# The second mixture of a gated four-layer block: eight dense experts replaced by 30 row tiles sorted by expert

## The chip, the cores and the metric

The kernel runs on one core of a Trainium2 chip. Its engines have programs of their own and meet at semaphores: TensorE (PE; its weight loads appear as PEld), VectorE (DVE), ScalarE (ACT), GpSimd (POOL), and SyncE (SP), which issues most of the DMAs in the order of its program. The metric is the device time of one execution in microseconds (us), the median of several.

## The reference

The input x has 4 batches of 256 tokens with 256 features (1024 tokens, eight row blocks of 128). Four layers follow each other; each adds a gated attention and a gated feed-forward part:

```
for l in 0..3:
    x = x + tanh(g_xattn[l]) * xattn_l(layernorm(x), ctx)
    x = x + tanh(g_ffn[l])   * ffn_l(layernorm(x))
```

The feed-forward part of layer 2 is the *second mixture* (all in f32, 8 experts, inner width H = 256, each token goes to its best 2):

```
r       = x * rsqrt(mean(x^2) + 1e-6) * rsqrt(256) * router_scale
logits  = r @ router_logits                      # 1024 x 8
choices = top 2 of logits; weights = probs / sum of the two chosen probs
for each token and each of its two experts e:
    y_e = (gelu(x @ gate_e) * (x @ up_e)) @ linear_e * per_expert_scale[e]
out = sum of weights_e * y_e
```

Only 2 of the 8 experts of a token enter the result. The attention of layer 3 (L3X) has self and cross parts; the feed-forward part of layer 3 is the last mixture, with 16 experts of inner width 128.

## The kernel before

Each engine has one long program, written out by hand, and the order of the work on an engine is the order of the code. An attention is a loop over steps t (from -8 on), run by `attention(f, fill)` on each engine; work of other stages is put beside it by a callback `fill(t)` that says at which step it stands. L2X, the attention of layer 2, has 64 units (steps 0 to 63 and some steps behind for what is late), L3X 128. SP's queue is in order too: an issue that waits for a semaphore holds back everything behind it.

The second mixture, L2F, is dense. `turn_part` (PE L1179) transposes the normed rows of a batch, `logits` (L1364) gives router logits of all 1024 tokens, DVE's `top2_mask` and `topk_weights` turn them into a weight for each token and expert. Then `experts` (PE L1374) computes all eight experts for all tokens. Each operand is split in two parts in a rounded format (hi and lo), and a product takes three matmuls (hi*hi, lo*hi, hi*lo). `first` (L1377, matmul L1392) makes gates and ups of an expert in 48 matmuls of 512 columns, `second` (L1399, matmul L1408) its down product in 48 matmuls of 256 columns. ACT applies the gelu (L2127), DVE multiplies (L2838) and adds each expert's share to x (L2853). Weights arrive by SP's `expert_weights` (L702) into two slots: a load waits until the matmuls of the expert before the last are done (`refill_first`, L720). POOL splits them (`split_weights`, L988; L1004 and L1007 for hi and lo). The norms that open L3X (`begin_late` on each engine, `part_moments`, `late_norms` on DVE) follow the last expert's sums, two of them between them.

The last mixture already works on rows sorted by expert, and its functions are the model of the new code. POOL scatters each row of the normed input by an indirect DMA to a place in a list per expert (`scatter`, L1142); the places come from ranks (PE matmuls, DVE `places`, L3328 to L3335). SP loads tiles of 128 rows from the lists (`rows`, L828), which are 260 wide: 256 features, the token's number, its first expert, its two weights. For each of 31 tiles PE transposes the rows (`tile_turn`, L1772), multiplies with f32 weights (`tile_gates`, L1790; `tile_down`, L1800), ACT copies, applies the gelu and weights the result (`tile_copy` L2449, `tile_gelu` L2459, `tile_out` L2469), DVE multiplies (`tile_prod`, L3438 to L3441) and POOL scatters the outputs (L1156). The 16 first tiles have an expert each; 15 later ones take expert and list block from registers that DVE's `tile_map` (L3406) fills. SP's loop there is

```
for j in range(TILE_RING, TILES):
    sp.wait_ge(fs["l3f"]["y_added"], YR + j - TILE_RING + 1)
    rows(j)
    if j - TILE_RING < LATER:
        later_weights(j - TILE_RING)
```

In L2X other work is put in: roundings of the next attention's weights (`HIGH_SELF`: eight on ACT, L2324, eight on DVE, L3198), the parked query weights of L3X (`park`), keys and values of the context (`keys_values`, PE L1218, called kv units: eight of them stand in the opening of L3X), and `low_self` on POOL, which splits L3X's output weights beside the experts. `keep_clock` (L1168) issues transposes that nothing reads.

Of the kernel before, what the change touches and what calls it, by code (L numbers as in the profile page):

```python
# [20 lines left out]
P = 128  # L21
# [161 lines left out]
L2F = Ffn("l2f", 2, 8, 128, 2, ACT.Gelu_apprx_tanh, False)  # L183
L3F = Ffn("l3f", 3, 2, 128, 1, ACT.Gelu, True, (8, 32, 32))
# [17 lines left out]
KV_LATE_AT = ((-6, -4, -3), (-5, -4, -4, -3, -3, -2))  # L202
# [22 lines left out]
PARTS = ((0, 4), (4, 6), (6, 8))  # L225
HIGH_SELF = [("k", 0, slice(0, 1024)), ("k", 1, slice(0, 1024)), ("q", 0, slice(0, 1024)), ("q", 1, slice(0, 1024)),
# [4 lines left out]
def build(nc, T, out, we_dram, kv_first, kv_cross, rows_in, rows_out, cross_q):  # L231
    ctx = ExitStack()
    with ctx:
# [73 lines left out]
        with ExitStack() as a:  # L307
            sb("tile_w_low_hold", [P, 64 * 256], where=a)
            tile_w += [sb(f"tile_w{i}", [P, n_w], where=a) for i in range(10, 15)]
            sb("more_w_low_hold", [P, 16 * 256 - 5 * n_w], where=a)  # L310
            more_w += [sb(f"more_w{i}", [P, n_w], where=a) for i in range(5, 10)]
        w_high, w_low = ({n: sb(f"w{n}_{part}", shape, F32R) for n, shape in wshapes} for part in ("high", "low"))
# [44 lines left out]
        with ExitStack() as a:  # L357

            with ExitStack() as a2:
                act_hi = [sb(f"act_hi{i}", [P, 2, NTOK], F32R, where=a2) for i in range(2)]  # L360
                act_lo = [sb(f"act_lo{i}", [P, 2, NTOK], F32R, where=a2) for i in range(2)]
# [123 lines left out]

        ps = [ctx.enter_context(nc.psum_tensor(f"ps{i}", [P, HALF], F32)) for i in range(8)]
# [34 lines left out]
        for f in (L1F, L2F):  # L521
            fs[f.name] = {k: sem(f"{f.name}_{k}") for k in
                          ("w13_in0", "w13_in1", "w2_in0", "w2_in1", "w13_split", "w2_split", "gu_ready",
                           "gated_ready", "prod_done", "hi_ready", "act_ready",
                           "y_ready", "y_added") if not (f is L1F and k == "y_added")}
        fs["l3f"] = {**fs["l2f"], "w13_hi": sem("l3f_w13_hi"), "w2_hi": sem("l3f_w2_hi")}
# [17 lines left out]
        n_keys = len(L2X.loads) + len(L3X.loads)  # L544

# [65 lines left out]
        def _(sp):  # L611
# [56 lines left out]
            def attention_weights(c):  # L668
# [17 lines left out]
                elif 14 <= c < 18:  # L686
                    quarter_of("o", c - 14, 1, lw["wo_in"])
# [13 lines left out]

            def expert_weights(f, free, value):  # L702

                s = fs[f.name]
                w13d, w2d = T[f.name + "_w13"], T[f.name + "_w2"]

                def w13_load(slot, e):
                    sp.dma_start(w13[slot][:, 0:KB * 2 * f.F * f.FB], w13d[bass.ds(e, 1)].rearrange(
                        "e p n -> p (e n)")).then_inc(s[f"w13_in{slot}"], 16)

                def w2_load(slot, e):
                    sp.dma_start(w2[slot][0:f.F, 0:f.FB, :], w2d[bass.ds(e, 1)].rearrange(
                        "e p k d -> p (e k) d")).then_inc(s[f"w2_in{slot}"], 16)

                sp.wait_ge(free, value)
                for slot in range(2):
                    w13_load(slot, slot)
                    w2_load(slot, slot)

                def refill_first(e):  # L720

                    slot = e[1]
                    sp.wait_ge(s["gu_ready"], (e[0] * 2 + slot + 1) * f.units)
                    w13_load(slot, e[0] * 2 + slot + 2)

                def refill_second(e):
                    slot = e[1]
                    sp.wait_ge(s["y_ready"], (e[0] * 2 + slot) * 4 + 4)
                    w2_load(slot, e[0] * 2 + slot + 2)


                refill_first((0, 0))
                with sp.Fori(0, f.E // 2 - 2) as i:
                    refill_first((i, 1))
                    refill_second((i, 0))
                    refill_first((i + 1, 0))
                    refill_second((i, 1))
                refill_first((f.E // 2 - 2, 1))
                refill_second((f.E // 2 - 2, 0))
                refill_second((f.E // 2 - 2, 1))  # L740

# [73 lines left out]
            def routed_weights():  # L815

                sp.wait_ge(lw["wo_lo"], 5)
# [5 lines left out]
            def routed_rows():  # L823
# [15 lines left out]
                sp.wait_ge(placed, 16 * CHOICES * NT)  # L839
# [15 lines left out]
            def load_got():  # L855

                for i in range(4):
                    sp.wait_ge(y_put[i], 16 * ((TILES + 3 - i) // 4))
                for t in range(0, NT, 2):
                    sp.dma_start(got[t // 2][:, t % 2, :, :], rows_out[t * P * CHOICES:(t + 1) * P * CHOICES, :].rearrange(  # L860
                        "(p k) d -> p k d", k=CHOICES)).then_inc(got_loaded(t)[0], 16)

# [10 lines left out]
            key_load(L2X, 4)  # L873
            key_load(L2X, 5)
            park(1)
            values_load(2)
            key_load(L2X, 6)
            park(2)
            key_load(L2X, 7)
            park(3)  # L880
            park(4)
            values_load(3)
            for p in range(5, PARKS):
                park(p)
            expert_weights(L2F, layer_done, 5)
# [29 lines left out]
        def _(pool):  # L915
# [139 lines left out]
            def low_self(i):  # L1055

                for h in range(8 * (i - 1), 8 * i, 2):
                    low = low_output(wsets[1]["o"], slice(h, h + 2), 1)
# [2512 lines left out]
```

## Time and profile before

| what | us |
|---|---|
| median of three runs (1389.11 to 1389.65) | 1389.5 |
| span of the profiled execution (no other time of it is recorded) | 1393.2 |
| L2X, end of it: last output matmuls | 612.3 |
| second mixture: first to last expert matmul | 620.4 to 755.9 |
| first scores of L3X | 788.0 |
| last mixture's tiles | 1320.6 to 1376 |

The span is cut in stages at these times. A row of the stage view gives, for each stretch, the busy time of every engine with its number of instructions, the clock granted to TensorE (1.00 is 2.4 GHz, 0.50 is 1.2 GHz), the mean busy share of the 16 DMA engines and the rate in GB/s. The profile's page counts 1301.3 us of TensorE busy (93% of the span), 986.2 of DVE, 817.6 of ACT and 683.2 of POOL. Its share of the chain that ended last is 73% for TensorE. An f32 matmul appears as two instructions, a transpose as one. In a timeline row the text in brackets tells how long the engine idled before and what ended that.

### The profile page before, as it was taken

To read this page: it belongs to the slowest core of one execution; us is meant where nothing else is said; L and a number is where in the kernel's file an instruction comes from. 1 tells how busy PE (TensorE), PEld (TensorE's weight loads), DVE (VectorE), ACT (ScalarE), POOL (GpSimd) and SP (SyncE) were. 2 spreads that over 40 slices of the span, in tenths; PEclk is the share of its full clock that TensorE was granted. 3 is DMA by queue.
4 is the path that set the end of the run, shared out by engine and by line. 5 is a ranking of instruction groups with operands and counts; after the bars stand their busy time and mean duration, and the time that the engine had idled before them with its cause. 6 is when DMAs were issued, how large, how long until landed. Compare 5 with 4: busy or idle time off the path is not lost.

```text
span 1393.2 us, 23503 instructions
## 1 busy us (share of the span) xinstructions
PE 1301.3 (93%) x7218; PEld 1087.1 (78%) x7218; DVE 986.2 (71%) x2337; ACT 817.6 (59%) x2029; POOL 683.2 (49%) x709
## 2 busy tenths in 40 slices
PE   6999999997899999989999799999999999999894
PEld 3556888885688888778887488888887888888783
DVE  7997556666877777745557577878778787876753
ACT  6964222334666767764222577776787777785363
POOL 1111555542343444434551246666777776765453
PEclk9999999999999999999999999999999999999897
DMA  6224555552201011011110594000321010032283
GB/s 234 83 95 125 167 183 166 166 185 68 85 32 61 32 53 39 1 46 39 49 42 23 164 335 122 1 1 17 84 107 32 31 62 31 32 128 98 95 299 105
DMA packets 73077, 129.42 MB, mean 93 GB/s; under 512 B 7381, under 2 KB 36713, under 8 KB 72460
## 3 DMA queue, kind: packets, MB, share of 16 engines
q1 hardware_dynamic: 67963, 118.66, 26.1%
q0 software_dynamic: 4432, 8.43, 1.9%
q8 instruction: 51, 0.84, 0.2%
q10 hardware_dynamic: 576, 1.05, 0.2%
q14 instruction: 55, 0.44, 0.1%
HBM read 86.75 MB, written 43.32 MB: 93 GB/s over the span
## 4 chain that ended last, share of the span: by engine, by line
PE 73%; DVE 12%; ACT 5%; issue 5%; POOL 3%; DMA 1%; SPq 0%; another core or an unknown queue 0%; POOLq 0%; ACTq 0%; DVEq 0%
PE ps L1448 9%; PE ps L1581 9%; PE ps L1554 9%; PE ps L1532 7%; PE ps L1599 7%; PE ps L1392 6%; PE ps L1564 5%; PE ps L1462 5%; PE ps L1543 3%; PE ps L1408 3%; PE ps L1218 3%; PE ps L1790 2%; POOL urs L955 2%; DVE usum L3063 1%; ACT probs L2237 1%
## 5 line engine op out<-in xcount | busy, mean ns | idle before, releaser
L962 POOL TENSOR_TENSOR probs<-probs,prec 128x512 f32<-128x512 f32 x192 | 202.3, 1054 | 284.8 <-DVE prec L3099 284.7
L2237 ACT ACTIVATE probs<-ps,nmax 128x256 f32<-128x256 f32 x384 | 178.8, 472 | 178.0 <-DVE nmax L3092 119.4
L1554 PE MATMUL ps<-k_feat,q_feat 128*128 128x256 f32 x768 | 198.4, 381 | 2.6 <-ACT q_feat L2227 1.9
L1581 PE MATMUL ps<-probs_t,v_tok 128*128 128x256 f32 x768 | 197.7, 380 | 0.2 <-ACT ob L2256 0.2
L955 POOL TENSOR_TENSOR urs<-uve,neg_half 128x4 f32<-128x4 f32 x136 | 137.0, 1007 | 55.5 <-DVE uve L3064 44.7
L1554 PEld LDWEIGHTS ps<-k_feat,q_feat 128*128 128x128 f32 x768 | 136.8, 190 | 16.8 <-issue 3.5
L1581 PEld LDWEIGHTS ps<-probs_t,v_tok 128*128 128x128 f32 x768 | 130.9, 190 | 10.6 <-ACT probs_t L2246 0.4
L1564 PE MATMUL ps<-ident,probs 128*128 128x128 f32 x768 | 116.3, 274 | 17.2 <-ACT probs_t L2246 16.3
L1564 PEld LDWEIGHTS ps<-ident,probs 128*128 128x128 f32 x768 | 92.1, 140 | 50.2 <-issue 22.4
L2246 ACT ACTIVATE probs_t<-ps 128x512 f32<-128x512 f32 x192 | 115.4, 601 | 0.9 <-PE ps L1564 0.9
L2156 ACT ACTIVATE gated<-ps 128x512 f32<-128x512 f32 x48 | 28.7, 598 | 136.0 <-PE ps L1448 134.0
L3092 DVE TENSOR_REDUCE nmax<-ps 128x2 f32<-128x512 f32 x128 | 87.1, 681 | 25.0 <-PE ps L1554 24.7
L1004 POOL TENSOR_TENSOR w_hi<-w,ones_col 128x512 fp32r<-128x512 f32 x37 | 43.5, 1176 | 115.5 <-DMA w<-in_l1f_w 51.0
L1543 PE MATMUL ps<-ident,uraw 128*128 128x128 f32 x544 | 82.9, 275 | 11.6 <-DVE uraw L3079 6.9
L935 POOL TENSOR_TENSOR rstd<-var_eps,neg_half 128x2 f32<-128x2 f32 x32 | 25.4, 797 | 138.1 <-DVE var_eps L2535 115.5
L1543 PEld LDWEIGHTS ps<-ident,uraw 128*128 128x128 f32 x544 | 68.0, 142 | 28.0 <-DVE uraw L3079 8.4
L3079 DVE TENSOR_TENSOR uraw<-ps,urs 128x512 f32<-128x512 f32 x80 | 55.3, 692 | 42.5 <-POOL urs L955 40.7
L2901 DVE TENSOR_TENSOR gated<-ps,gated 128x512 f32<-128x512 f32 x48 | 33.2, 691 | 71.2 <-ACT gated L2156 71.1
L970 POOL TENSOR_TENSOR o_e<-of,om 128x256 fp32r<-128x256 bf16 x120 | 81.4, 699 | 0.0
L1599 PE MATMUL ps<-wo_high,o_e 128*128 128x256 f32 x256 | 80.0, 336 | 0.0
L1448 PE MATMUL ps<-h_hi,w_hi 128*128 128x512 f32 x192 | 76.4, 398 | 1.4 <-ACT kv_out L1949 0.7
L2237 ACT ACTIVATION_READ_ACCUMULATOR probs<-ps,nmax 128x1 f32 x384 | 76.6, 199 | 0.0
(429 smaller groups left out, 3686.4 us busy)
## 6 DMA issues: line engine op xcount, KB each, us to landing
rows_in<-zero_rows SPq DMA_DIRECT2D x3, 5200.0 KB, 35.2
tile_w<-in_l3f_w SPq DMA_DIRECT2D x21, 385.5 KB, 7.1
w<-in_l1f_w SPq DMA_DIRECT2D x24, 256.0 KB, 5.2
spread_w<-we_dram SPq DMA_DIRECT2D x16, 384.0 KB, 3.6
kv_cross<-kv_out SPq DMA_DIRECT2D x20, 256.0 KB
kv_first<-kv_out SPq DMA_DIRECT2D x16, 256.0 KB
spread_w<-we_dram SPq DMA_DIRECT2D x16, 256.0 KB, 4.1
w<-in_l2f_w SPq DMA_DIRECT2D x8, 512.0 KB
```

The source lines that it names most:

```text
L955: pool.tensor_tensor(urs[r % 2][:, :], uve[r % 2][:, :], neg_half[:, 0:4], ALU.pow).then_inc(s["rs_ready"], 1)
L962: pool.tensor_tensor(p3, p3, spread(prec[g % 3][:, :], [P, TB, S]), ALU.mult)\
L1448: mm = pe.matmul(ps[2 * g + half][:, :], w[:, kb, g, :], h[:, kb, half * HALF:(half + 1) * HALF], start=kb == 0 and q == 0, stop=kb == KB ...
L1532: mm = pe.matmul(ps[f.bank(p)][:, :], x_in_[:, kb, :], w[:, kb, n * HALF:(n + 1) * HALF], start=kb == 0 and q == 0, stop=kb == KB - 1 and ...
L1543: mm = pe.transpose(ps[5][:, i * P:(i + 1) * P], uraw[r % f.ring][:, i * P:(i + 1) * P], ident[:, :])
L1554: mm = pe.matmul(ps[g % 2][:, j * S:(j + 1) * S], q_feat[:, h, j * P:(j + 1) * P], k_feat[:, kv, :], start=True, stop=True)
L1564: mm = pe.transpose(ps[4][:, tb * S + j * P:tb * S + (j + 1) * P], probs[g % 4][:, j, tb * P:(tb + 1) * P], ident[:, :])
L1581: mm = pe.matmul(ps[6][:, 0:S], v_tok[:, tb, kv * P:(kv + 1) * P], probs_t[g % 2][:, tb, :], start=tb == 0, stop=tb == TB - 1)
L1599: mm = pe.matmul(ps[7][:, j * D:(j + 1) * D], lhs, w, start=h == 0 and j == 0 and q == 0, stop=h == HEADS - 1 and j == TB - 1 and q == len ...
L2237: ins = act_e.activation(probs[g % 4][:, j, :], ps[g % 2][:, j * S:(j + 1) * S], ACT.Exp, bias=nmax[g % 3][:, j:j + 1], **kw, accum_out=ps ...
L2246: act_e.activation(probs_t[g % 2][:, :, :].rearrange("p a s -> p (a s)"), ps[4][:, :], ACT.Copy).then_inc(s["pt_out"], 1)
L3092: v.tensor_reduce(nmax[g % 3][:, :], bank, AX.X, ALU.max, negate=True)\
```

## The change

The dense experts, their weight splits, and the splits of the normed input go. In their place stand 30 f32 tiles of 128 rows, in two lists. List one holds batches 0 to 2 (19 tiles: one per expert with its weights loaded ahead into a buffer of its own, and 11 later tiles with the expert chosen by register), list two batch 3 (8 fixed tiles and 3 later). Eight row buffers (`MID_RING`) and four weight buffers for later tiles (`MID_SETS`) are used in turn. Rows are 260 wide (130 KB a tile), an expert's weights 1536 f32 per partition (768 KB).

The router, ranks and places of batches 0 to 2 move into L2X's steps 50 to 68, with eight DMAs that fill the lists with zero rows between SP's parks, and the eight fixed weight loads at its end. POOL scatters eight times in steps 65 to 68, four times after the loop and four times (batch 3) between the tiles' output scatters at j = 11 to 14. The roundings of `HIGH_SELF` move from L2X to the tile loop (ACT j = 12 to 19, DVE j = 13 to 20). The outputs of the tiles are scattered to DRAM, loaded again (`load_mid_got`) and added to x (`mid_add`): for batches 0 to 2 beside list two, with their norms for L3X (moments at j = 24 to 26, turns at PE's j = 29 to 31); for batch 3 in L3X's steps 0 to 7. Three of the kv units stand ahead of the tiles, two behind them, three in L3X's steps -7, -5 and -4. The output weights of L3X are loaded behind the tiles and split in L3X's steps 2 to 10 (ACT high, POOL low).

The core of the diff (SP's tile loop, PE's tile loop, the steps of PE in L2X and the removed calls):

```diff
-            expert_weights(L2F, layer_done, 5)
-            store_kv(len(KV_ALL) - KV_GAPS[2], len(KV_ALL), kv_late)
+            mid_fixed_weights()
+            mid_tiles()
...
+                def rows(j):
+                    which, n = mid_list(j)
+                    block = MID_BASE[which] + n * MID_BLOCKS[which] if n < MID else blocks[mid_later(j)]
+                    if j >= MID_RING:
+                        sp.wait_ge(*mid_at("act", j - MID_RING + 1))
+                    sp.dma_start(mid_x[j % MID_RING][:, :], mid_rows[bass.ds(block, 1)].rearrange("n p d -> p (n d)"))\
+                        .then_inc(mid_rows_loaded(j)[0], 16)
...
+                def later(i):
+                    if i >= MID_SETS:
+                        sp.wait_ge(*mid_at("down", mid_tile_of(i - MID_SETS) + 1))
+                    sp.dma_start(mid_more_w[i % MID_SETS][:, :], T["l2f_w"][bass.ds(experts_of[i], 1)].rearrange(
+                        "e p n -> p (e n)")).then_inc(mid_weights_loaded(mid_tile_of(i))[0], 16)
...
+                sp.wait_ge(*mid_at("placed", 16 * CHOICES * 3 * TB))
+                for j in range(MID_RING):
+                    rows(j)
+                experts_of, blocks = registers(0)
+                sp.wait_ge(s["out_ready"], L2X.total)
+                for i in range(MID_SETS):
+                    later(i)
+                store_kv(len(KV_ALL) - KV_GAPS[2], len(KV_ALL) - KV_GAPS[2] + KV_WITH_MID, kv_late)
+                first_b = MID_TILES[1][0]
+                for j in range(MID_RING, first_b):
+                    rows(j)
+                    i = j - MID_RING - 3 + MID_SETS
+                    if MID_SETS <= i < MID_LATER[0]:
+                        later(i)
+                sp.wait_ge(*mid_at("placed", 16 * CHOICES * NT))
+                for j in range(first_b, first_b + MID):
+                    rows(j)
...
-            logits(wg2, 8, 0, 3 * TB)
-            keep_clock(8, 6)
-            turn_part(SECOND_LN, 3, h_tok, quantised, SECOND_LN * B, ps[5])
-            pe.wait_ge(part_out, SECOND_LN * B + 4)
-            logits(wg2, 8, 3 * TB, NT)
-            experts(L2F)
+            def mid_turn(j):
+                pe.wait_ge(*mid_rows_loaded(j))
+                if j >= 2:
+                    pe.wait_ge(*mid_at("copied", j - 1))
+                for kb in range(KB):
+                    mm = pe.transpose(ps[j % 2][:, kb * P:(kb + 1) * P], mid_x[j % MID_RING][:, kb * P:(kb + 1) * P],
+                                      ident[:, :])
+                mm.then_inc(mid_signal("turned"), 1)
+            def mid_gates(j):
+                pe.wait_ge(*mid_at("copied", j + 1))
+                pe.wait_ge(*mid_weights_loaded(j))
+                if j >= 2:
+                    pe.wait_ge(*mid_at("act", j - 1))
+                w = mid_weights(j)[:, 0:MID_GU].rearrange("p (k g f) -> p k g f", k=KB, g=2)
+                for g in range(2):
+                    for fb in range(2):
+                        for kb in range(KB):
+                            at_ = (2 * g + fb) * P
+                            mm = pe.matmul(ps[2 + j % 2][:, at_:at_ + P], w[:, kb, g, fb * P:(fb + 1) * P],
+                                           mid_feat[j % 2][:, kb, :], start=kb == 0, stop=kb == KB - 1)
+                mm.then_inc(mid_signal("gates"), 1)
...
+            keys_values(KV_WITH_MID, ps[0:2])
+            pe.wait_ge(kv_copied, kv_done[0])
+            pe.wait_ge(at["l2x"]["o_out"], L2X.total)
+            mid_turn(0)
+            for j in range(MID_ALL + 2):
+                if j + 1 < MID_ALL:
+                    mid_turn(j + 1)
+                if j < MID_ALL:
+                    mid_gates(j)
+                if j == 2:
+                    pe.wait_ge(at["l2x"]["y_added"], B)
+                if j == 4:
+                    turn_part(SECOND_LN, 3, h_mid, quantised, SECOND_LN * B, ps[4])
+                if j == 6:
+                    mid_logits(2)
+                if j == 10:
+                    mid_ranks(2)
+                if j >= MID_ALL - 1:
+                    b = j - MID_ALL + 1
+                    turn_part(LAST_LN, b, h_late, quantised, (LAST_LN - 1) * B + b + 1, ps[4 + b % 2])
+                if j >= 2:
+                    mid_down(j - 2)
+            pe.wait_ge(*mid_at("out", MID_ALL))
+            keys_values(KV_LATE_FIRST[1], ps[0:2])
```

`mid_down(j)` is two matmuls of 256 columns over the two halves of the inner width. POOL's loop scatters tile j when ACT has weighted it; ACT's `mid_weighted(j)` waits for the output scatter of tile j - 4.

## Rows read from the trace of the kernel before

**Rows 1.** By stages: us, busy of five engines, granted clock, DMA share, GB/s

```profile
324.00:612.30 288.30, 271.12 (x1422) 228.49 (x1420) 209.67 (x592) 196.66 (x509) 114.06 (x110) 0.99 0.13 45
...
620.40:755.90 135.50, 135.31 (x768) 119.18 (x768) 79.14 (x171) 43.53 (x71) 65.00 (x54) 0.99 0.12 35
755.90:788.00 32.10, 25.58 (x95) 14.21 (x93) 19.18 (x55) 18.17 (x35) 7.20 (x8) 1.00 0.18 66
...
1320.60:1376.00 55.40, 50.59 (x373) 45.01 (x372) 26.62 (x130) 33.10 (x93) 27.48 (x28) 1.00 0.59 200
```

**Rows 2.** Chain of waits, one expert of the mixture: start, us, work

```profile
650.37 10.91 PE ps L1392 x48
661.27 5.75 PE ps L1408 x48
```

**Rows 3.** Timeline of TensorE, tiles of the last mixture: start, us

```profile
1325.43 0.38 PE L1772 MATMUL ps<-ident,tile_x 128*128 128x128 f32 x2
1325.65 1.06 PE L1790 MATMUL ps<-tile_feat,tile_w 128*128 128x128 f32 x8
1326.54 0.60 PE L1800 MATMUL ps<-tile_w,tile_act 128*128 128x256 f32 x2
1326.98 0.38 PE L1772 MATMUL ps<-ident,tile_x 128*128 128x128 f32 x2
```

**Rows 4.** Groups of instructions, 1320.6 to 1376: count, busy, mean ns, idle before

```profile
L1156 POOL DMA_INDIRECT rows_out<-tile_y,tile_to x28 | 27.5, 982 | 34.1 <-ACT tile_y L2469 23.4 <-issue 10.6
...
L2469 ACT ACTIVATE tile_y<-ps,tile_wt 128x256 f32<-128x256 f32 x31 | 14.6, 474 | 6.4 <-PE ps L1800 2.6 <-DMA rows_out<-tile_y,tile_to 2.0 <-issue 0.9
```

**Rows 5.** Waits of TensorE, last steps of L2X: total, times, longest

```profile
PE ps L1564 <- ACT probs_t L2246: 4.6, 7, 1.5
```

**Rows 6.** Timeline of TensorE, step 63 of L2X

```profile
598.52 1.03 PE L1554 MATMUL ps<-k_feat,q_feat 128*128 128x256 f32 x4
```

**Rows 7.** Timeline of VectorE, places of four row blocks

```profile
1282.95 0.23 DVE L3328 TENSOR_TENSOR slot_of<-ps,list_at 128x64 f32<-128x64 f32 x1
...
1284.52 0.17 DVE L3335 CAST place<-place_f 128x8 uint32<-128x8 f32 x1
```

**Rows 8.** Timeline of GpSimd, row scatters of the last mixture

```profile
1296.21 0.96 POOL L1142 DMA_INDIRECT rows_in<-h_near,place  x1 [0.30 <-issue]
...
1312.46 0.96 POOL L1142 DMA_INDIRECT rows_in<-h_near,place  x1 [0.30 <-issue]
```

**Rows 9.** Timeline of SP's queue, row loads of the last mixture

```profile
1314.97 3.18 SPq L828 DMA_DIRECT2D tile_x<-rows_in  x7
```

**Rows 10.** Timeline of SP's queue, third expert's gate weights

```profile
633.23 0.33 SPq L708 DMA_DIRECT2D w<-in_l2f_w  x1
```

**Rows 11.** Timeline of GpSimd, first split of these weights

```profile
636.85 1.51 POOL L1004 TENSOR_TENSOR w_hi<-w,ones_col 128x512 fp32r<-128x512 f32 x1 [7.89 <-DMA w<-in_l2f_w]
```

**Rows 12.** DMA issues: count, KB each, median us to landing

```profile
v_tok<-kv_cross SPq DMA_DIRECT2D x8, 512.0 KB, 3.7
...
cross_q<-park_high SPq DMA_DIRECT2D x8, 256.0 KB, 2.0
...
wo_raw<-in_l3c_o SPq DMA_DIRECT2D x1, 2048.0 KB, 8.3
```

**Rows 13.** Short windows around an idle time of TensorE, columns as rows 1

```profile
330.00:331.00 1.00, 0.00 (x0) 0.00 (x0) 0.97 (x2) 0.96 (x2) 0.37 (x1) 0.96 0.75 231
331.00:332.00 1.00, 0.00 (x0) 0.00 (x0) 0.38 (x2) 1.00 (x3) 0.51 (x1) 0.50 1.02 387
...
337.50:338.00 0.50, 0.50 (x4) 0.39 (x3) 0.31 (x1) 0.50 (x2) 0.00 (x0) 0.76 0.00 0
```

**Rows 14.** Timeline of TensorE, restart after that idle time

```profile
333.29 1.12 PE L1543 MATMUL ps<-ident,uraw 128*128 128x128 f32 x4 [4.71 <-DVE uraw L3079]
```

**Rows 15.** Chain of waits, opening of L3X

```profile
782.95 1.72 PE ps L1218 x4
...
787.98 1.12 PE ps L1554 x4
```

More of the change, by code:

```diff
@@ L201 @@
 KV_GAPS = (4, 4, 8)
[L202 removed]
+KV_LATE_AT = ((-6, -4, -3), (-7, -5, -4))
 KV_LATE_FIRST = (1, 2)
@@ new lines, in _ @@
+            run(attention(L2X, beside_l2x))
+            pool.wait_ge(*mid_at("places", 2))
+            mid_scatter(4)
+            part_scales(1)
+            root_mean_square(2)
+            for j in range(MID_ALL):
+                pool.wait_ge(*mid_at("out", j + 1))
+                pool.indirect_dma_start(mid_out[:, :], bass.IndirectOffsetOnAxis(ap=mid_to[:, j:j + 1], axis=0),
+                                        mid_y[j % 4][:, :], None, bounds_check=CHOICES * NTOK - 1,
+                                        oob_is_err=False).then_inc(mid_signal(f"put{j % 4}"), 16)
+                if j == 11:
+                    pool.wait_ge(*mid_at("places", 4))
+                if 11 <= j < 15:
+                    mid_scatter(1)
+                if j in (22, 23, 24):
+                    part_scales(1)
@@ new lines, in _, with mid_logits @@
+            packed_experts(L1F)
+            keys_values(KV_LATE_FIRST[0], ps[0:2])
+            turn_late(FIRST_LN, 0, h_tok)
+            def mid_logits(part):
+                first, last = PARTS[part]
+                pe.wait_ge(part_out, SECOND_LN * B + last // TB)
+                for t in range(first, last):
+                    at_ = MID_LOGITS_AT[part] + (t - first) * MID
+                    for kb in range(KB):
+                        mm = pe.matmul(ps[MID_LOGITS_BANK[part]][:, at_:at_ + MID], h_feat[:, kb, t * P:(t + 1) * P], wg2[:, kb, :],
+                                       start=kb == 0, stop=kb == KB - 1)
+                mm.then_inc(logits_ready, 1)
@@ new lines, in mid_ranks @@
+            def mid_ranks(part):
+                first, last = PARTS[part]
+                nt = last - first
+                pe.wait_ge(*mid_at("const", 1))
+                pe.wait_ge(*mid_at("masks", part + 1))
+                bank = ps[5][:, MID_RANKS_AT[part]:MID_RANKS_AT[part] + (nt + 1) * MID]
+                r = bank.rearrange("p (t e) -> p t e", e=MID)
+                masks = mid_best[:, first:last, :]
+                pe.matmul(bank, mid_ones[:, :], mid_no_ranks[:, 0:(nt + 1) * MID], start=True, stop=False)
+                pe.matmul(r[:, 0:nt, :], mid_before[:, :], masks, start=False, stop=False)
+                for t in range(nt):
+                    mm = pe.matmul(r[:, t + 1:nt + 1, :], mid_ones[:, :],
+                                   masks[:, t:t + 1, :].to_broadcast([P, nt - t, MID]), start=False,
+                                   stop=t == nt - 1)
+                mm.then_inc(mid_signal("ranks"), 1)
@@ new lines, in mid_down @@
+            def mid_down(j):
+                pe.wait_ge(*mid_at("act", j + 1))
+                if j >= 2:
+                    pe.wait_ge(*mid_at("out", j - 1))
+                w = mid_weights(j)[:, MID_GU:MID_W].rearrange("p (k d) -> p k d", k=2)
+                for fb in range(2):
+                    mm = pe.matmul(ps[6 + j % 2][:, 0:D], mid_act[:, j % 3, fb * P:(fb + 1) * P], w[:, fb, :],
+                                   start=fb == 0, stop=fb == 1)
+                mm.then_inc(mid_signal("down"), 1)
@@ new lines, in toward_mid, with mid_copy @@
+                if t in (63, 66):
+                    mid_exp((63, 66).index(t))
+            run(attention(L2X, toward_mid))
+            act_e.wait_ge(parked, 32 * PARKS)
+            keys_values(KV_WITH_MID, ps[0:2], kv_late)
+            def mid_copy(j):
+                act_e.wait_ge(*mid_at("turned", j + 1))
+                act_e.activation(mid_feat[j % 2][:, :, :].rearrange("p k t -> p (k t)"), ps[j % 2][:, 0:D],
+                                 ACT.Copy).then_inc(mid_signal("copied"), 1)
```

946 lines of the change are left out of this document (555 added, 391 removed).

## The prediction

> **What bounds the kernel now.** I read the span by stages first [rows 1]. In the stretch of the second mixture, 620.4 to 755.9 us, TensorE is busy for 135.31 of 135.5 us at granted clock 0.99, and the DMA share is 0.12: the stage is TensorE's alone. The chain of waits says the same [rows 2]: each expert stands on it with 48 gate matmuls of 512 columns in 10.91 us and 48 down matmuls in 5.75 us, 16.66 us each, 8 x 16.66 = 133.3 us. Whatever replaces this stage is judged by how long TensorE is kept, and by what it waits for. The last mixture already works as the new one will: its tiles show what an f32 tile costs TensorE [rows 3] and the other engines [rows 4].
>
> **The sum is made against the profiled execution**, whose span is 1393.2 us; the three runs have their median at 1389.5, 3.7 us lower. I work out differences on the profile's times and put them on the median.
>
> **1. TensorE's work: cheaper.** In [rows 3] two transposes take 0.22 us (1325.43 to 1325.65), eight gate instructions 0.89 (0.111 each), two down instructions 0.44. A new tile has an inner width of 256 instead of 128: the same two transposes, 16 gate and 4 down instructions. 0.22 + 1.78 + 0.87 = 2.87 us, and 30 tiles make 86 us. That is 49 us less than the 135.5 of the dense stage. ACT weights a tile's outputs in 0.47 us and POOL scatters them in 0.98 [rows 4]; ACT's copy and gelu of the same 128x256 cost no more each, so neither engine reaches 2.87: they hide under TensorE.
>
> **2. The end of L2X: zero.** The eight big weight roundings leave ACT there, and TensorE's waits for ACT's probs_t, 4.6 us in all [rows 5], may shrink; but router logits, rank matmuls and three turns now come before the last outputs. I take zero between -4.6 and +3. The zero rows (8.8 MB) and the fixed weights (6.3 MB) go into a stage with DMA share 0.13 [rows 1]; hidden. SP does them in its order between the parks, so if that cover fails the parks and the scatters after them are late: up to +3.
>
> **3. The first tile: late by 3.8.** A tile can start only when rows of three batches are placed. Scores of step 63 start at 598.52 [rows 6]; ranks come some 3.5 us later, the places bundle takes 1.74 us (1282.95 to 1284.69 [rows 7]), the marked rows about 1.5: scatters from 605. There are 12, each 0.96 with 0.30 of issue before it [rows 8], 15.2 us: 620.3. After the last one of the last mixture (1312.46 + 0.96) SP's row loads went out 1.55 us later [rows 9], and such a load lands in some 2.3: 624.2. The dense stage began at 620.41, so +3.8 (bounds 0 and +8: POOL also has attention's work in these steps). Three context-key units of 1.72 us [rows 15] stand in the gap, free.
>
> **4. The later weights: the wait that decides.** Eight tiles of list one have fixed weights; eleven take theirs by register into four buffers. From the fifth of these on, SP waits for the down matmuls of the tile that has the buffer, then issues the weights (768 KB) and then, behind them on the same queue, the next tile's rows (130 KB). In the loop, at j = 11 SP issues rows 11, then waits for down of tile 8; TensorE issues that at the end of its step 10. Rows 12 are queued behind the wait, and TensorE's step 11 begins with the transposes of tile 12. The weights themselves have a step in hand, the rows none. So in steps 11 to 17, seven times, TensorE stands from its own down matmul until 898 KB have landed, because SP's next wait is released only by the step that this one starts. Nothing hides it: gates and down matmuls are in order behind the transposes.
>
> What one such wait costs: in the dense stage SP's 512 KB load went out at 633.23 [rows 10], right after the matmuls that free the buffer, and POOL, which had waited 7.89 us for it, began on the data at 636.85 [rows 11]: 3.62 us. 386 KB more cost (8.3 - 3.7) / 1536 KB = 3.0 us per 1024 KB [rows 12], 1.16, and the second issue adds a little: X = 4.85 us. Bounds: 4.2 if half of the added bytes overlap the fixed part, and 5.6 = 3.62 + 2.0 if the rows behave like a transfer of their own behind the weights [rows 12].
>
> **5. The clock in these gaps.** In an idle time of 4.71 us before 333.29 [rows 14] the granted clock had fallen to 0.50 (1.2 GHz) by 331, and it was back at 2.4 GHz only around 337.6 [rows 13], 4.3 us after the restart. Gaps of 4.85 us lie in the same place. A burst of 2.87 us of full-speed work then runs some 4.4 us at half speed (2.2 done) and the rest full: about 4.9 to 5.1; I take 4.9. Period P = 4.85 + 4.9 = 9.75, bounds 7.1 (4.2 + 2.87) and 11.3 (5.6 + 2 x 2.87).
>
> The Trainium skill, page "TensorE: Matmul & The Clock Gate", section "HAM oscillation — how this bites in real kernels", describes this shape: matmul bursts shorter than the transfer each waits for, so that every burst starts at the low clock. It speaks against this change. The row at 331 agrees for one such gap; seven in a row stand in no trace here.
>
> **6. The stage.** From 624.2: steps 0 to 10 are 11 x 2.87 = 31.6, 4 for the first tile's pipeline and a cold start, 2 for the fourth batch's turn, logits and ranks: 661.8. Seven steps of 9.75 make 68.3: 730.1. Steps 18 to 29 are 12 x 2.87 = 34.4; their rows are not behind a wait, for the fourth batch is placed by then. 2.5 for the last outputs and the clock's return: 767.0. Against 755.9, list stage and late start are +11.1 together.
>
> **7. The opening of L3X: 6.8 back.** It took 32.1 us with TensorE busy for 25.58 [rows 1], up to the first scores at 787.98 [rows 15]. Three of its eight key units (1.72 each, 5.2 us) moved in front of the tiles, and three of four norms lie beside list two, some 1.6 more: 25.3 us. Bounds: 20 (25.58 - 5.2, no wait left) and 32.1 (DVE sets it anyway).
>
> **8. Early L3X: +1.2**, for the fourth batch's norm, its sums and eight output-weight splits on POOL that were beside the experts (bounds 0 and +4).
>
> Sum: +11.1 - 6.8 + 1.2 = +5.5, so 1395 us. The saving of 49 us at TensorE is spent by seven exposed transfers (7 x 4.85 = 34), their slow bursts (7 x 2 = 14) and the start.
>
> **Rivals.**
> A: the clock does not pay. Seven gaps leave it high, or the bursts run at full speed: P = 4.85 + 2.87 = 7.7, 54 us, 14.2 less, 1381: faster than before. For it: the clock stayed full for some 2 us of the idle time of [rows 14], so a gap that is somewhat shorter than X loses little. Against: X, as worked out, is as long as that idle time. It decides from P = 8.95 downwards (7 x 0.8 = 5.5).
> B: the rows are not late, because SP runs ahead in a way that I misread: 7 x 2.87 = 20 instead of 68, 1347. Against: the order in the loop.
> C: bursts wholly at half speed, P = 4.85 + 5.74 = 10.6 (+5.9), and the first rows of list two late for the fourth batch's scatters, which stand in POOL's queue between output scatters (+5): 1406. For: scatters of the last mixture queue one behind the other, 0.3 of issue each [rows 8].
> The section of the Trainium skill's page "TensorE: Matmul & The Clock Gate" named above draws each burst as slow, as C has it; [rows 13] show the low clock ending within one longer burst.
>
> **How the numbers follow.** Forecast 0.50, A 0.20, B 0.10, C 0.20. The forecast's own range is 1386 to 1404, from the bounds of X, of the start and of the opening. 0.2% is 2.8 us, about what these runs can tell from nothing: same is 1386.7 to 1392.3. Faster: A 0.18, B 0.10, the low end of the forecast 0.06: 0.34. Same: 0.12 of the forecast and 0.02 of A: 0.14. Slower: 0.32 and C, 0.52. The range 1371 to 1412 leaves out B and a tenth of C and A.
>
> **What would show it.** Right: seven idle times of TensorE of 4 to 5.6 us, 7 to 11 us apart, each ended by the rows' transfer and the granted clock at 0.50 behind them; tiles of 2.87 us before and after; first tile near 624; first L3X scores some 25 us after the last tile. Wrong: idle times that end on something else, a period of 2.87 throughout (B), clock 1.00 in the bursts (A), or a stretch of L3X changed by more than 4 us.

## The result, and the profile after

The changed kernel takes 1404.0 us (median of four runs, 1401.3 to 1405.0) beside 1389.6 of the kernel before: ratio 1.0095, 95% interval 1.008 to 1.011. It is slower by 14.4 us, 1%; forecast were 5.5 us, 1395 in a range of 1371 to 1412, with a chance of 0.52 for slower. The profiled execution took 1401.3 us, its span is 1399.6.

The stages after, in the columns of [rows 1] (busy PE, PEld, DVE, ACT, POOL, granted clock, DMA share, GB/s):

```profile
612.80:625.40 12.60, 4.91 (x12) 1.92 (x11) 6.28 (x30) 1.79 (x3) 8.21 (x10) 0.81 0.33 107
625.40:660.70 35.30, 35.25 (x256) 33.07 (x256) 12.15 (x66) 16.90 (x38) 7.85 (x8) 0.92 0.53 180
660.70:730.50 69.80, 36.00 (x157) 32.46 (x157) 18.19 (x74) 15.06 (x29) 10.71 (x11) 0.71 0.35 118
730.50:769.40 38.90, 37.30 (x282) 34.69 (x280) 25.05 (x92) 20.05 (x47) 16.48 (x17) 1.00 0.39 136
769.40:793.60 24.20, 19.46 (x65) 11.61 (x65) 13.67 (x31) 12.37 (x22) 5.94 (x6) 0.93 0.55 195
793.60:1280.00 486.40, 463.91 (x2714) 397.92 (x2715) 374.45 (x776) 363.64 (x978) 331.31 (x374) 0.99 0.26 83
```

In place of the dense stage's 135.5 us [rows 1] stand 12.6 up to the first tile (of which TensorE waits 7.7) and 35.3 + 69.8 + 38.9 of tiles; the opening of L3X is 24.2 instead of 32.1. The middle stretch is the one to look at: TensorE is busy for 36.0 of 69.8 us, at a mean clock of 0.71. Its timeline shows every idle time there with what ended it:

```profile
625.41 1.09 PE L1866 MATMUL ps<-ident,mid_x 128*128 128x128 f32 x4 [7.70 <-DMA mid_x<-mid_rows]
...
665.68 0.69 PE L1866 MATMUL ps<-ident,mid_x 128*128 128x128 f32 x2 [4.96 <-DMA mid_x<-mid_rows]
...
674.70 0.44 PE L1866 MATMUL ps<-ident,mid_x 128*128 128x128 f32 x2 [4.64 <-DMA mid_x<-mid_rows]
...
684.29 0.69 PE L1866 MATMUL ps<-ident,mid_x 128*128 128x128 f32 x2 [4.86 <-DMA mid_x<-mid_rows]
...
694.41 0.69 PE L1866 MATMUL ps<-ident,mid_x 128*128 128x128 f32 x2 [4.84 <-DMA mid_x<-mid_rows]
...
704.49 0.69 PE L1866 MATMUL ps<-ident,mid_x 128*128 128x128 f32 x2 [4.73 <-DMA mid_x<-mid_rows]
...
714.76 0.69 PE L1866 MATMUL ps<-ident,mid_x 128*128 128x128 f32 x2 [4.85 <-DMA mid_x<-mid_rows]
...
725.09 0.69 PE L1866 MATMUL ps<-ident,mid_x 128*128 128x128 f32 x2 [4.92 <-DMA mid_x<-mid_rows]
...
730.29 0.38 PE L1866 MATMUL ps<-ident,mid_x 128*128 128x128 f32 x2
730.51 1.95 PE L1881 MATMUL ps<-mid_feat,mid_more_w 128*128 128x128 f32 x16
732.29 1.03 PE L1892 MATMUL ps<-mid_more_w,mid_act 128*128 128x256 f32 x4
733.16 0.38 PE L1866 MATMUL ps<-ident,mid_x 128*128 128x128 f32 x2
```

Seven idle times of 4.64 to 4.96 us, each ended by a row tile's landing, stand between bursts of one tile each. Behind them, from 730.29 to 733.16, a tile takes 2.87 us, the figure worked out from [rows 3]. SP's queue at one of these steps: the weights go out when TensorE's down matmuls end (709.91), and the rows behind them.

```profile
710.08 0.33 SPq L1002 DMA_DIRECT2D mid_more_w<-in_l2f_w  x1
710.60 0.33 SPq L995 DMA_DIRECT2D mid_x<-mid_rows  x1
```

The two kinds of transfer (count, KB each, median us from issue to landing):

```profile
mid_more_w<-in_l2f_w SPq DMA_DIRECT2D x14, 768.0 KB, 4.3
...
mid_x<-mid_rows SPq DMA_DIRECT2D x30, 130.0 KB, 3.1
```

And the clock across one gap and its burst:

```profile
709.90:714.80 4.90, 0.05 (x2) 0.04 (x1) 1.42 (x5) 1.51 (x2) 1.96 (x2) 0.80 0.67 227
714.80:716.00 1.20, 1.20 (x6) 1.20 (x7) 0.00 (x0) 0.38 (x1) 0.00 (x0) 0.50 0.00 0
...
718.00:719.00 1.00, 1.00 (x6) 1.00 (x5) 0.00 (x0) 0.10 (x1) 0.00 (x0) 0.50 0.00 0
719.00:720.20 1.20, 1.17 (x4) 0.59 (x2) 0.88 (x2) 0.29 (x1) 0.00 (x0) 0.74 0.00 0
```

The clock falls inside the idle time (0.80 on average), is at its low level (0.50, 1.2 GHz) from the burst's first instruction to 719.0 at least, 4.2 us behind it, and rises inside the last window (0.74). In [rows 13] the low level lasted some 4.3 us behind the restart.

### The profile page after: what moved, and what is told of

It reads as the page before. It is cut to its first block, busy times and chain, and to the rows that moved or that the text cites. A ratio compares the mean times of both kernels' runs of the same rounds, so it can differ in the third digit from the quotient of the medians.

```text
span 1399.6 us, 23540 instructions
## 1 busy us (share of the span) xinstructions
PE 1272.7 (91%) x7122; PEld 1067.1 (76%) x7122; DVE 965.6 (69%) x2457; ACT 814.7 (58%) x2055; POOL 671.1 (48%) x720
## 4 chain that ended last, share of the span: by engine, by line
PE 69%; DVE 12%; issue 6%; ACT 4%; DMA 4%; POOL 4%; SPq 0%; ACTq 0%; POOLq 0%; DVEq 0%
PE ps L1609 9%; PE ps L1741 9%; PE ps L1714 8%; PE ps L1692 7%; PE ps L1759 7%; PE ps L1623 5%; PE ps L1881 5%; PE ps L1724 5%; PE ps L1703 3%; PE ps L1442 3%; DMA mid_x<-mid_rows 2%; POOL urs L1147 2%; PE ps L1892 2%; DVE usum L3242 1%; PE ps L2046 1%
## 5 line engine op out<-in xcount | busy, mean ns | idle before, releaser
L2382 ACT ACTIVATE gated<-ps 128x512 f32<-128x512 f32 x48 | 28.8, 599 | 135.5 <-PE ps L1609 135.5
L3271 DVE TENSOR_REDUCE nmax<-ps 128x2 f32<-128x512 f32 x128 | 87.1, 681 | 25.7 <-PE ps L1714 25.3
L1703 PE MATMUL ps<-ident,uraw 128*128 128x128 f32 x544 | 83.3, 276 | 12.5 <-DVE uraw L3258 7.4
L1703 PEld LDWEIGHTS ps<-ident,uraw 128*128 128x128 f32 x544 | 68.3, 143 | 29.0 <-DVE uraw L3258 9.3
L1284 POOL DMA_INDIRECT mid_out<-mid_y,mid_to x30 | 29.9, 997 | 108.0 <-ACT mid_y L2581 106.5
L2453 ACT ACTIVATE q_feat<-ps,qcols 128x512 f32<-128x512 f32 x96 | 73.9, 770 | 3.9 <-PE ps L1703 3.9
```

The lines of the kernel that those rows point to most:

```text
L1703: mm = pe.transpose(ps[5][:, i * P:(i + 1) * P], uraw[r % f.ring][:, i * P:(i + 1) * P], ident[:, :])
L3271: v.tensor_reduce(nmax[g % 3][:, :], bank, AX.X, ALU.max, negate=True)\
```

## The experiments

Times are medians where no single run is named; the kernel before ran beside each and stayed at 1389.3 to 1389.7.

**Rows further ahead.**

```diff
-                    i = j - MID_RING - 3 + MID_SETS
+                    i = j - MID_RING - 5 + MID_SETS
                     if MID_SETS <= i < MID_LATER[0]:
                         later(i)
+                for i in range(first_b - MID_RING - 5 + MID_SETS, MID_LATER[0]):
+                    later(i)
```

> SP issues the row loads two tiles further ahead of the weight loads that wait (rows 13 before the first waiting weights, instead of rows 11). Theory one (the rows are late only because they stand behind a waiting weight load on SP's queue): the seven idle times of about 4.8 us go; weights then have one step of lead, so a step of TensorE is bounded by some 3.3 us ((3.9 + 2.65) / 2) instead of 9.9, no gap is long enough for the clock to fall, and the time is 7 x 6.6 = 46 us shorter than the changed kernel: about 1358, between 1353 and 1366. Rival (the weights themselves are the limit, since each of four buffers comes free only by the down matmuls of an earlier tile): the idle times stay above 3 us, now ended by the weights at the gate matmuls, and under 20 us are gained: 1385 or more.

Measured: 1368.2 us (1364.0 to 1370.1), ratio to before 0.984 (0.982 to 0.986). The seven idle times are gone; what TensorE still waits for in the tile loop (wait: total, times, longest; one of the two waits for rows is the first tile's 7.8):

```profile
PE ps L1868 <- DMA mid_x<-mid_rows: 13.2, 2, 7.8
PE ps L1883 <- issue: 3.0, 2, 1.6
PE ps L1883 <- ACT mid_feat L2566: 2.1, 1, 2.1
```

So the order on the queue was the cause, as theory one has it, and 36 of the 46 us came: the time lies just above the expected 1353 to 1366. The rest: three gate groups wait 1.5 to 2.1 us, and list two's first rows are late. The profile puts two of the three waits down to issue, that is to nothing it shows, and one to ACT's copy; that they are waits for weights is read from SP's queue, where these tiles' weights went out 4.4 to 5.0 us before their gate matmuls began, and a load of 768 KB took 4.2 us or more. So the seven steps took 26.3 us (662.31 to 688.65) and not 7 x 3.3 = 23; with 5.4 of waiting for list two's rows and 1.5 more in the slow burst behind it, these are the missing 10 us. The next fences are TensorE's idle time, POOL's last row scatter of the fourth batch, and SP's queue, which sends the rows out when that scatter is done:

```profile
694.00 0.69 PE L1868 MATMUL ps<-ident,mid_x 128*128 128x128 f32 x2 [5.35 <-DMA mid_x<-mid_rows]
```

```profile
688.09 0.96 POOL L1241 DMA_INDIRECT mid_rows<-h_mid,mid_place  x1 [0.30 <-issue]
```

```profile
681.10 4.91 SPq L1002 DMA_DIRECT2D mid_more_w<-in_l2f_w  x2
690.59 8.35 SPq L995 DMA_DIRECT2D mid_x<-mid_rows  x8
```

That was half of rival C's mechanism; in the changed kernel the seven stalls gave these scatters their time.

**TensorE kept busy in the gaps, first try.**

```diff
+                if 11 <= j < 18:
+                    keep_clock(40, 4)
                 if j + 1 < MID_ALL:
                     mid_turn(j + 1)
```

> 40 transposes of the identity, whose product nothing reads, stand on TensorE ahead of the wait for rows in steps 11 to 17 of the tile loop: some 4.4 us at full clock in gaps of 4.8. Theory (the bursts after the gaps take 4.4 to 5.4 us instead of 2.87 because the clock has fallen to 1.2 GHz): granted clock 1.00 in the stretch, bursts of 2.9, gaps as long as before with the transposes in them, 14 to 16 us gained: about 1389. Rival (bursts are long because of the transfers beside them or of waits inside them): no gain, bursts stay at 4.4 to 5.4, 1404 +- 2.

Measured: 1413.7 us, slower by 10. I had priced a product with the identity like a transpose (0.11 us). But `keep_clock` issues matmuls with the identity (`pe.matmul`, L1168 of the kernel before), not transposes, as the description of the kernel before and the expectation have it. As an f32 matmul such a product is two instructions, 0.223 us, and 40 of them fill 8.9 us, more than the gap. TensorE has no idle time in these steps, and its clock is 1.00 (the first filling with the transposes behind it, then the stretch):

```profile
661.77 9.09 PE L1392 MATMUL ps<-ident 128*128 128x128 f32 x80
670.70 0.38 PE L1866 MATMUL ps<-ident,mid_x 128*128 128x128 f32 x2
```

```profile
661.00:745.00 84.00, 84.00 (x724) 83.13 (x724) 18.11 (x74) 16.38 (x31) 10.69 (x11) 1.00 0.31 100
```

**19 products instead of 40.**

> The run with 40 identity products had 8.9 us of them in each step (0.223 us each: f32 products take two instructions where a transpose takes one), more than the gap, so it was slower although the clock stayed at 1.00. Here 19 stand in each of the seven gaps: 4.2 us in gaps of 4.85. Theory (the low clock makes the bursts 4.4 to 5.4 us): bursts of 2.9, clock 1.00, 7 x 2.87 = 20.1 instead of 36.0 us of bursts, 14 to 16 gained: 1389, 1386 to 1392. Rival (bursts are long for another reason): 1404.

Measured: 1386.4 us (1384.0 to 1388.0, eight runs), 17.6 less than the changed kernel and faster than before (0.997, 0.996 to 0.999). The stretch of the seven steps, and two of its idle times:

```profile
661.00:716.00 55.00, 51.08 (x420) 48.98 (x419) 17.58 (x73) 14.86 (x28) 10.70 (x11) 1.00 0.41 143
```

```profile
681.45 0.44 PE L1866 MATMUL ps<-ident,mid_x 128*128 128x128 f32 x2 [0.41 <-DMA mid_x<-mid_rows]
...
689.17 0.44 PE L1866 MATMUL ps<-ident,mid_x 128*128 128x128 f32 x2 [0.38 <-DMA mid_x<-mid_rows]
```

A step is 7.7 to 8.0 us now (7.72 from 681.45 to 689.17, the shortest): the transfer as before, and a burst of 2.87. Seven of them take 55.2 us where the changed kernel's profile has 69.6: 14.3 of the 17.6 us are seen in these steps and are the low clock's. The other 3.3 are not; executions of one kernel differ by that much, as the account below has it. This run is what rival A described, somewhat slower than its 1381 at a period of 7.7.

**Weights in two loads, released by the matmuls that read each; rows further ahead; the fourth batch's scatters together.** Three changes in one run, of which the second widens that of the first experiment.

```diff
+                def later_gu(i):
+                    if i >= MID_SETS:
+                        sp.wait_ge(*mid_at("gates", mid_tile_of(i - MID_SETS) + 1))
...
+                def later_dn(i):
+                    if i >= MID_SETS:
+                        sp.wait_ge(*mid_at("down", mid_tile_of(i - MID_SETS) + 1))
...
                     rows(j)
-                    i = j - MID_RING - 3 + MID_SETS
-                    if MID_SETS <= i < MID_LATER[0]:
-                        later(i)
+                    if MID_SETS <= j - MID_RING < MID_LATER[0]:
+                        later_gu(j - MID_RING)
+                    if MID_SETS <= j - MID_RING - 2 < MID_LATER[0]:
+                        later_dn(j - MID_RING - 2)
...
-                if j == 11:
+                if j == 10:
                     pool.wait_ge(*mid_at("places", 4))
-                if 11 <= j < 15:
-                    mid_scatter(1)
+                    mid_scatter(4)
```

> Each later tile's weights come in two loads: the gate and up part (512 KB) waits for the gate matmuls of the tile that had the buffer, the down part (256 KB) for its down matmuls; rows stand ahead of both, by two and four tiles more than in the changed kernel; the fourth batch's four row scatters stand together at POOL's j = 10. In the run with rows ahead alone (1368) three gate groups still waited 1.5 to 2.1 us for weights and list two's first rows 5.4 us for the fourth batch's scatters. Theory: with these gone a tile takes 2.87 us throughout, the seven steps 20 us instead of 70, 14 us less than with rows ahead alone: 1354, 1350 to 1360. Rival (transfers of 0.9 MB per tile are the limit by now): a period above 3.2 us in the later tiles, 1362 or more.

Measured: 1352.6 us (1350.2 to 1355.9), ratio to before 0.974 (0.972 to 0.976). TensorE's waits for rows are the first tile's 7.7 and one of 1.0, and 20.0 us in the steps that had the gaps hold 20.0 us of work:

```profile
PE ps L1887 <- DMA mid_x<-mid_rows: 8.8, 2, 7.7
```

```profile
657.00:677.00 20.00, 20.00 (x159) 19.08 (x158) 15.42 (x70) 15.38 (x28) 10.62 (x9) 1.00 0.92 301
```

The rival did not happen: with rows and weights for every tile a tile takes 2.87 us, while 301 GB/s were moved at a DMA share of 0.92. What each of the three changes gave of the 15.6 us beyond the run with rows ahead was not tried. Of the 51.4 us between this run and the changed kernel, the seven steps' 69.6 - 20.1 = 49.5 are the exposed transfers and their slow bursts.

**The kernel before, once more.**

> The kernel before, unchanged, with another profile. The first profile of it has a span of 1393.2 us while its runs have a median of 1389.5; the changed kernel's profile lies 1.7 below its own run. Theory: the first profile caught an execution some 5 us longer than most, in its last stage: here the span is about 1387.8, and from the last scores of L3X to the end it takes about 120.6 us instead of 126.2, as in the changed kernel. Rival: the last stage takes 126 here too, so the change itself made it 5.6 us shorter.

Measured: span 1388.1, run 1389.9. From the last scores of L3X (1267.65) to the end it takes 120.5 us, where the first profile has 126.2 and the changed kernel 120.6. The theory holds: that profile was 5 us long in its last stage. The change left that stage alone, and this profile is the one to compare L3X with. Between first and last scores of L3X the two profiles of the kernel before have 479.0 and 478.4 us, so differences below some 0.6 say nothing here.

**Where L3X loses.** First and last scores of L3X in the kernel before (second profile), and in the changed one:

```profile
789.26 1.10 PE L1554 MATMUL ps<-k_feat,q_feat 128*128 128x256 f32 x4 [1.01 <-ACT q_feat L2227]
...
1267.65 1.03 PE L1554 MATMUL ps<-k_feat,q_feat 128*128 128x256 f32 x4
```

```profile
793.62 1.10 PE L1714 MATMUL ps<-k_feat,q_feat 128*128 128x256 f32 x4 [1.01 <-ACT q_feat L2453]
...
1279.00 1.03 PE L1714 MATMUL ps<-k_feat,q_feat 128*128 128x256 f32 x4
```

478.4 us became 485.4. Three runs asked why.

*The fourth batch's norm without the mixture's sums, beside list two:*

```diff
-                if j in (22, 23, 24):
+                if j in (22, 23, 24, 25):
                     part_scales(1)
...
                 if j in (24, 25, 26):
                     mid_add(j - 24)
+                if j in (24, 25, 26, 27):
                     part_moments(LAST_LN, j - 24)
-                if j in (26, 27, 28):
+                if j in (26, 27, 28, 29):
                     part_shift(LAST_LN, j - 26)
...
-                if t == 0:
-                    mid_add(3)
-                    part_moments(LAST_LN, 3)
-                if t == 3:
-                    part_shift(LAST_LN, 3)
```

> Leaves out the addition of the second mixture to the fourth batch, so that its moments, shift and scales can be taken beside list two and not in L3X's steps 0 to 3. What counts is L3X's length from its first to its last scores: 478.4 to 479.0 us in two profiles of the kernel before, 485.4 in the changed one. Theory B (the two sums, moments and aggregates of VectorE, 2.8 us on the chain at step 0, and what follows from them): 482 to 483, a third to half of the 6.7 us back. Rival A (the weight splits on ACT and POOL cost nearly all): above 484.

Measured (one run, 1399.5 us): L3X 483.5 us, 1.9 back.

```profile
793.96 1.10 PE L1714 MATMUL ps<-k_feat,q_feat 128*128 128x256 f32 x4 [1.01 <-ACT q_feat L2453]
...
1277.43 1.03 PE L1714 MATMUL ps<-k_feat,q_feat 128*128 128x256 f32 x4
```

*The weight splits at steps 9 to 23 instead of 2 to 10* (`t in (9, 13, 17, 21)` on ACT, `(10, 11, 14, 15, 18, 19, 22, 23)` on POOL):

> The split of L3X's output weights (four ACT copies of 1.05 us, eight POOL subtractions of 1.28 us) moves from steps 2 to 10 of L3X to steps 9 to 23. Between the first scores of L3X and its step 27 or so the changed kernel loses 6.2 us against the kernel before. Theory A (these twelve instructions stand in chains of ACT and POOL that TensorE waits for): about 4 of the 6.2 come back: 1400. Rival B (the fourth batch's sums and moments on VectorE at step 0 are what delays the start of L3X, and the splits hide): within 1 us of 1404.

Measured: 1403.2 us (1401.5 to 1405.5), L3X 485.5: no gain. The run alone spoke for rival B. But its seventh group of scores came 26.9 us behind the first, not 30.0 as in the changed kernel; this lead of 3.1 us was gone 121 us behind the first scores. The splits now stand from 41 to 102 us behind them.

*The splits left out:*

```diff
-            for n in range(4):
-                sp.dma_start(wsets[1]["o"][:, 4 * n:4 * n + 4, :], T["l3s_o"][:, 4 * n:4 * n + 4, :])\
-                    .then_inc(lw["wo_in"], 16)
+            sp.sem_inc(lw["wo_in"], 64)
...
-                    act_e.activation(w_high["o"][:, part, :], wsets[1]["o"][:, part, :], ACT.Copy)\
-                        .then_inc(lw["wo_hi"], 1)
+                    act_e.sem_inc(lw["wo_hi"], 1)
...
-                    low = low_output(wsets[1]["o"], slice(2 * i, 2 * i + 2), i // 2 + 1)
```

> Leaves out the split of the self part's output weights in L3X (their load, four ACT copies, eight POOL subtractions); the two tiles that the output matmuls read are filled with zeros by POOL right behind the tile loop. What counts is L3X from its first to its last scores: 478.4 us before, 485.4 changed, 483.5 without the fourth batch's sums, 485.5 with the splits at steps 9 to 23. Theory A (what is left of the 7 us after the sums' 1.9 is the splits): 480 to 481. Rival C (neither; something else in L3X, such as SP's order or the key units, slows it): 484 or more. The opening may be longer by the filling.

Measured (one run, 1400.2 us): L3X 480.2 us, 5.1 back. The filling with zeros made the opening 2.7 us longer (26.2 us from its first key unit to the first scores, not 23.5), which this length leaves out.

```profile
798.00 1.10 PE L1717 MATMUL ps<-k_feat,q_feat 128*128 128x256 f32 x4 [1.01 <-ACT q_feat L2456]
...
1278.24 1.03 PE L1717 MATMUL ps<-k_feat,q_feat 128*128 128x256 f32 x4
```

1.9 + 5.1 = 7.0 of 7.0: what the two runs give back adds up to the loss; no run left out both. Moving the splits to later steps had not taken them out of the way: L3X lost as much there. Whether ACT's copies or POOL's subtractions weigh more was not tried.

**The splits in the opening** (ACT at steps -3 to -1, POOL at -3 to 0, their load ahead of the fourth batch's):

> The split of L3X's output weights on ACT and POOL moves from steps 2 to 10 into the opening (ACT at steps -3 to -1, POOL at -3 to 0), behind loads that are issued ahead of the fourth batch's. In the run with the splits at steps 9 to 23 the first 24 scores of L3X came some 3 us earlier, and it was lost again later. Theory A (POOL's 10.3 us and ACT's 4.3 stand in chains wherever TensorE is not the bound): L3X from first to last scores 480 to 482 instead of 485.4, the opening 1 to 3 us longer, net 1 to 4 us gained: about 1401. Rival (the splits cost nothing, batch four's sums do): L3X at 485, opening longer, 1405.

Measured: 1402.6 us (1399.8 to 1403.9). L3X 482.6, 2.8 less; from the opening's first key unit to the first scores 24.5 us instead of 23.5. Net 1.8 over these two stretches, 1.4 by the medians; the ranges of the runs overlap, so it can't be told from nothing.

**Both together:**

> The version with weights in two loads (1352.6) together with the weight splits in the opening of L3X, which alone gave 1402.6 beside 1404 of the changed kernel. Theory (the two act in different stages and add): 1351, 1348 to 1353. Rival (with the tile loop shorter the output weights arrive no earlier against the opening, and the splits delay it by what L3X gains): 1352 to 1354, no difference.

Measured: 1351.2 us (1350.5 to 1355.8), ratio to before 0.973 (0.971 to 0.975), the lowest of all; against 1352.6 it can't be told apart.

## Why the prediction was right, and where it was not

Its steps, with the changed kernel's profile beside them:

1. *TensorE's work per tile*, 2.87 us: 2.87.
2. *The end of L2X at zero*: TensorE goes on from its last output matmuls to the next work at 612.4, before at 612.1. At most 0.5 us was lost there, the zero rows and fixed weights included.
3. *The first tile at 624.2*: 625.4. Scatters began at 606.6 (605 by the sum), 1.27 apart as in [rows 8].
4. *The exposed transfer, X = 4.85 us, seven times*: 4.96, 4.64, 4.86, 4.84, 4.73, 4.85, 4.92, together 33.8 where the sum had 34. Built on one load of the dense stage [rows 10, 11] and the slope of [rows 12], this was the term the forecast hung on, and the run with rows ahead shows that its cause is the order on SP's queue. The mechanism was right; that the mean of 4.83 agrees to 0.02 is luck, for the bounds were 4.2 and 5.6.
5. *Bursts of 4.9 us*: 4.4, 4.7, 5.3, 5.4, 5.4, 5.4, 5.2, together 35.8 against 34.3. That the clock is the reason is shown by the 19 products: the seven steps got 14.3 us shorter, where step 5 had priced 14. Each burst ended at a higher clock (0.74 in the last window of the burst shown), so the price is 2.2 us a burst and not the full 2.87. The Trainium skill, page "TensorE: Matmul & The Clock Gate", section "HAM oscillation — how this bites in real kernels", has every burst start at the low clock when its wait is longer than it. Six of the seven bursts here agree; the second began at 1.00, and its clock fell inside it (last section).
6. *The stage*: seven steps 69.6 us (68.3 forecast); steps 0 to 10 in 35.3 (37.6, the cold start cost less), the rest 39.1 to the cut at 769.4 (36.9: the turns of three batches and 1.6 us of waiting for ACT at 768.08 were not in it). The last down matmul ends at 769.6, forecast 767.0.
7. *The opening*, 25.3 us: 24.2. First scores of L3X at 793.6; 792.3 by the sum. The errors of steps 3 to 7, 1.1 to 2.3 us each and of both signs, cancel to 1.3 here, which is luck too. Against the second profile of the kernel before, each counted from its first scores in L2X (before, then changed), this point lies 5.5 us later; the sum had +4.3.

```profile
351.01 1.10 PE L1554 MATMUL ps<-k_feat,q_feat 128*128 128x256 f32 x4 [0.87 <-ACT q_feat L2227]
```

```profile
349.86 1.10 PE L1714 MATMUL ps<-k_feat,q_feat 128*128 128x256 f32 x4 [0.87 <-ACT q_feat L2453]
```

8. *Early L3X, +1.2 with bounds 0 and +4*: here the prediction failed in size. It cost 7.0, above the upper bound. The prediction itself had named a stretch of L3X changed by more than 4 us as a sign of being wrong, and this sign came. The step counted the fourth batch's norm and the weight splits as mostly covered, and named POOL's eight subtractions but not ACT's four copies. They were not covered: TensorE is not the bound in L3X's first steps. In 20 us from 12 us behind the first scores it was busy for 17.4 to 17.5 in the kernel before and for 15.7 in the changed one. The clock does not make the difference: it was 0.91 and 1.00 in the two profiles of before, and 0.91 after (before in its first and second profile, then after):

```profile
800.00:820.00 20.00, 17.49 (x93) 15.13 (x94) 14.73 (x34) 14.59 (x39) 9.75 (x10) 0.91 1.09 334
```

```profile
801.26:821.26 20.00, 17.41 (x101) 14.74 (x101) 15.94 (x35) 14.92 (x40) 10.75 (x11) 1.00 1.09 335
```

```profile
805.60:825.60 20.00, 15.68 (x79) 12.81 (x79) 14.90 (x35) 14.48 (x35) 12.94 (x12) 0.91 1.09 335
```

Of the rest of the 14.4: 5.5 to the first scores and 7.0 in L3X make 12.5. The second profile of before and the profile of after lie 11.5 us apart as runs (1389.9 and 1401.3), since the latter started its first scores 1.15 us earlier; it was the fastest of its four runs. The other 3 us are differences between executions. Part of them can lie in the bursts: the seven steps took 69.6 us in this profile, but 71.8 and 72.5 in those of the two runs with the splits moved (to steps 9 to 23, and into the opening), whose code of these steps is the same. There the first two bursts too took over 5 us, where this profile has 4.4 and 4.7. With the splits at steps 9 to 23, the transposes behind the first idle time and those behind the last burst:

```profile
666.30 0.69 PE L1866 MATMUL ps<-ident,mid_x 128*128 128x128 f32 x2 [4.85 <-DMA mid_x<-mid_rows]
...
733.26 0.38 PE L1866 MATMUL ps<-ident,mid_x 128*128 128x128 f32 x2
```

The rivals. A did not happen, and the run with 19 products shows that it would have turned the sign, as it was said: at a period of 7.7 to 8.0 the kernel is faster than before. B did not happen; the order of the loop was read rightly. C's all-cold bursts did not happen in this profile (5.7 forecast, 5.1 on average; with the splits in the opening the first two bursts took 5.8), and its late rows of list two only came out once the stalls were gone. The sign was right because of steps 4 and 5, which make 70 us of what is 20 us of work: the whole saving of 49 us went there. With saving and loss equal, the sign itself hung on the smaller terms, of which the late first tile is 5 us and the wrongly sized step 8 another 7. The size was not right: 14.4 us against 5.5. That 1404 lies in the range of 1371 to 1412 owes something to the width of that range; the forecast's own, 1386 to 1404, just ends there.

## What to carry to other kernels

On an in-order queue, ask for each issue that waits what stands behind it, and when that is needed: here 130 KB of rows that were ready stood behind a weight load that had a step in hand, and the same transfers in another order took 36 us less. Free a buffer in the parts in which it is read, so that the first part can be loaded when its last reader is done; the run that did this, with two other changes, had no wait for weights left. And work that is moved into a stretch where TensorE waits for other engines is not hidden by TensorE's length elsewhere: here 5.1 us came of splits that keep POOL for 10.3 and ACT for 4.3, and 1.9 of sums and moments of 2.7 on VectorE. Test it by leaving it out, since moving it may only move the cost.

## What the runs showed of the hardware

An identity product in f32 took 0.223 us (80 instructions from 661.77 to 670.70 in the run with 40), twice a transpose of a tile of that size (0.11, [rows 3]), so the same number of them is worth twice the time as filler. TensorE kept its clock at 1.00 through seven gaps that were filled to 0.4 to 0.7 us of idle time, and ran at 0.50 for most of each burst behind the gaps of 4.6 to 5.0 us. In one of these gaps the fall came late: the clock was 1.00 to the end of the idle time before 674.70 and fell inside the burst (changed kernel, windows of that gap and burst):

```profile
672.00:674.70 2.70, 0.00 (x1) 0.01 (x1) 0.29 (x2) 0.00 (x0) 0.31 (x1) 1.00 0.70 276
674.70:676.00 1.30, 1.30 (x9) 1.30 (x10) 0.00 (x0) 0.38 (x1) 0.00 (x0) 0.71 0.00 0
676.00:677.50 1.50, 1.50 (x9) 1.50 (x9) 0.00 (x0) 0.00 (x0) 0.00 (x0) 0.50 0.00 0
```

Two profiled executions of the kernel before differed by 5.7 us in their last stage alone (126.2 and 120.5), as much as the whole forecast difference: a single profile is not a base to measure such a difference against.
